# Spreading dt and du over the state rows: four DMAs of 32 channels over 128 partitions, or four DMAs of 128 channels over 32 partitions

## The reference

```python
def selective_scan(u, dt, Bm, Cm, A, Dp):
    def step(h, inp):
        u_t, dt_t, B_t, C_t = inp
        dA = jnp.exp(dt_t[..., None] * A)
        h = h * dA + (dt_t * u_t)[..., None] * B_t[:, None, :]
        y = jnp.einsum('bdn,bn->bd', h, C_t)
        return (h, y)
    ...
dt = jax.nn.softplus(x_dbl[..., :R] @ dt_w.T + dt_b)
Bm = x_dbl[..., R:R + N]
Cm = x_dbl[..., R + N:]
```

## Time and profile before

| what | us |
|---|---|
| median of 3 runs | 606.04 |
| profiled execution | 607.73 |
| its span | 605.9 |
| GpSimd busy | 517.9 (85%) |
| VectorE busy | 483.3 (80%) |
| TensorE busy | 480.8 (79%) |
| ScalarE busy | 357.5 (59%) |
| SP's DMA queue, share of 16 DMA engines | 47.6% |

### The profile page before, as it was taken

One profiled execution on the slowest core, in us unless ns is written; L12 is line 12 of the kernel. 1 busy time (PEld: TensorE's weight loads), 2 busy tenths in 40 slices (PEclk: granted clock), 3 DMA queues, 4 the chain that ended last, 5 costly groups with the idle time before them and its releaser, 6 DMA issues.

```text
span 605.9 us, 5758 instructions
## 1 busy us (share of the span) xinstructions
PE 480.8 (79%) x1679; PEld 177.7 (29%) x1679; DVE 483.3 (80%) x601; ACT 357.5 (59%) x634; POOL 517.9 (85%) x190
## 2 busy tenths in 40 slices
PE   2576858777788888869888888878887887888897
PEld 1232212232323232314232323232333223323243
DVE  2533069998989896999899889988998899799941
ACT  2454565758585856483857485848574764354533
POOL 5737159999999999999999999999999999989600
PEclk9997958899999897998998999999999998789999
DMA  6839458855555546564644864386429741900000
GB/s 66 33 32 183 84 133 199 192 148 123 152 121 147 130 141 138 144 140 143 138 110 116 190 159 108 98 189 178 109 78 187 195 114 45 207 3 10 9 1 17
DMA packets 51073, 71.32 MB, mean 118 GB/s; under 512 B 16434, under 2 KB 17378, under 8 KB 51042
## 3 DMA queue, kind: packets, MB, share of 16 engines
q1 hardware_dynamic: 48050, 69.63, 47.6%
q0 software_dynamic: 1024, 1.05, 4.5%
q10 hardware_dynamic: 1968, 0.29, 0.3%
HBM read 60.45 MB, written 10.49 MB: 117 GB/s over the span
## 4 chain that ended last, share of the span: by engine, by line
POOL 33%; issue 26%; PE 18%; DVE 15%; ACT 5%; DMA 2%; POOLq 0%; DVEq 0%; ACTq 0%
POOL st L464 16%; POOL st L455 12%; DVE st L1350 9%; DVE st L1337 3%; PE ps L580 2%; PE ps L640 2%; PE ps L646 2%; POOL l_ L441 2%; POOL dt L444 2%; DMA x<-in_L_tok_ple_table,idx 2%; PE ps L627 2%; PE ps L732 2%; PE ps L748 2%; POOL x L429 1%; PE ps L568 1%
## 5 line engine op out<-in xcount | busy, mean ns | idle before, releaser
L464 POOL TENSOR_TENSOR st<-st,repC 128x2048 f32<-128x2048 f32 x63 | 284.9, 4533 | 9.1 <-ACT carry L998 7.8
L1350 DVE TENSOR_TENSOR_SCAN st<-ps,carry,st 128x512 f32<-128x512 f32 x192 | 234.9, 1268 | 19.6 <-ACT carry L998 12.9
L992 ACT ACTIVATE ps<-dtS,negA 128x512 f32<-128x512 f32 x256 | 169.5, 681 | 51.8 <-DVE st L1350 50.4
L455 POOL TENSOR_TENSOR st<-duS,repB 128x2048 f32<-128x2048 f32 x31 | 140.5, 4531 | 0.5 <-PE ps L646 0.5
L640 PE MATMUL ps<-Bw,nought 128*128 128x512 f32 x194 | 103.6, 645 | 0.0
L646 PE MATMUL ps<-st,fold 128*32 128x512 f32 x504 | 69.5, 624 | 42.9 <-POOL st L464 42.7
L1350 DVE TENSOR_TENSOR_SCAN st<-ps,zero,st 128x512 f32<-128x512 f32 x64 | 78.1, 1267 | 3.8 <-POOL st L455 1.9
L1337 DVE TENSOR_TENSOR st<-duS,ps 128x2048 f32<-128x2048 f32 x33 | 75.0, 2271 | 6.3 <-PE ps L627 6.3
L580 PE MATMUL ps<-act,wT 128*128 128x512 f32 x128 | 62.4, 633 | 5.2 <-ACT act L943 5.2
L998 ACT ACTIVATE carry<-st 128x4 f32<-128x4 f32 x48 | 9.8, 204 | 77.7 <-DVE st L1350 77.5
L640 PEld LDWEIGHTS ps<-Bw,nought 128*128 128x128 f32 x194 | 35.6, 202 | 50.0 <-issue 49.9
(11 more groups left out here) (129 smaller groups left out, 590.4 us busy)
## 6 DMA issues: line engine op xcount, KB each, us to landing
dtS<-dt_dram SPq DMA_DIRECT2D x64, 256.0 KB, 6.9
duS<-du_dram SPq DMA_DIRECT2D x64, 256.0 KB, 4.6
repC<-bc_dram SPq DMA_DIRECT2D x64, 256.0 KB, 5.7
repB<-bc_dram SPq DMA_DIRECT2D x60, 128.0 KB, 2.9
dt_dram<-dt SPq DMA_DIRECT2D x16, 256.0 KB, 2.1
du_dram<-du SPq DMA_DIRECT2D x16, 256.0 KB, 2.0
bc_dram<-bc_sb SPq DMA_DIRECT2D x16, 64.0 KB, 5.5
out_h<-fin SPq DMA_DIRECT2D x8, 128.0 KB, 2.0
```

The costliest lines, as they stand in the source:

```text
L455: pool.tensor_tensor(st[:, r], duS[:, u % 2], row, ALU.mult).then_inc(sem("dbu_pool"), 1)
L464: pool.tensor_tensor(st[:, r], st[:, r], row, ALU.mult).then_inc(sem("hc_ready"), 1)
L992: sc.activation(decay_bank(u, r, q), dtS[:, u % 2, q], ACT.Exp, scale=negA[:, way(u), q, r:r + 1]).then_inc(sem("decay_ready"), 1)
L1350: dve.tensor_tensor_scan(st[:, r, q, order], decay_bank(u, r, q)[:, order], st[:, r, q, order], first, ALU.mult, ALU.add).then_inc(sem("sc ...
```

## The change

`load_dt` and `load_du` still issue four DMAs of 256 KB each for a unit. Before, the DMA for m writes all 128 channels (as 32 x 4 x 512) to the 32 partitions of that m. After, the DMA for q writes the 32 channels of that group to all 128 partitions, four copies of 32 rows; the source is a view of the DRAM rows with a leading dimension of 4 and step 0. The destination has 128 rows of 512 numbers. Waits, semaphores, buffers and the order of all instructions on all engines stay the same, and so do the bytes moved and the length of a contiguous piece (2 KB).

```diff
+            def four_times(of, u, q):
+
+                return of[u][32 * q:32 * q + 32].unsqueeze(0).broadcast_to([4, 32, T])
+
             def load_dt(u):
                 wait(sp, "decay_ready", NQ * NR * (u - 1))
                 sp.wait_ge(sem("dt_in_dram"), 16 * (u + 1))
-                for m in range(4):
-                    sp.dma_start(dtS[32 * m:32 * m + 32, u % 2], dt_dram[u].rearrange("(q d) t -> d q t", d=32)) \
-                      .then_inc(sem(f"dtS_in_{u % 2}"), 16)
+                for q in range(NQ):
+                    sp.dma_start(dtS[:, u % 2, q, :], four_times(dt_dram, u, q)).then_inc(sem(f"dtS_in_{u % 2}"), 16)
 
             def load_du(u):
                 ...
                 sp.wait_ge(sem("du_in_dram"), 16 * (u + 1))
-                for m in range(4):
-                    sp.dma_start(duS[32 * m:32 * m + 32, u % 2], du_dram[u].rearrange("(q d) t -> d q t", d=32)) \
-                      .then_inc(sem(f"duS_in_{u % 2}"), 16)
+                for q in range(NQ):
+                    sp.dma_start(duS[:, u % 2, q, :], four_times(du_dram, u, q)).then_inc(sem(f"duS_in_{u % 2}"), 16)
```

## The result

The changed kernel takes 697.72 us (median of 4 runs, 695.65 to 698.55), the kernel before on the same chip 606.21 us: 1.1506 times as long, 95% interval 1.148 to 1.1532. The profiled execution has a span of 696.1 us. The prediction was 761, range 648 to 915.

What follows compares the result with a forecast made beforehand. GpSimd bounds the kernel at 30.9 us a unit; on four engines SP's chain takes over. Unit 2's du loads at 128, 13 units of 41.5, 29.6 to dt's landing and 63.7 to the end give 761 us, range 648 to 915.

Steps and rivals of the forecast that it cites:

- GpSimd at 30.9 us a unit, 27 us of slack: Middle units: GpSimd's work sets 30.9 us a unit; readers of dtS and duS come some 27 us after the loads.
- The smaller side decides, four engines, the same four: New dt and du loads: source leads with 4, so each runs on the same 4 engines, 256 packets a unit; 84%.
- 31 missing small packets: SP's queue before: 5345 small packets against 336 x 16 = 5376, fitting three parameter DMAs with fewer than 16 rows.
- B: Rival on the new loads: all 16 engines are used and nothing changes, 606 us within 0.2%; chance 11%.
- C: Rival on the loads of units 0 and 1: all 16 engines and faster, at most 2 us gained, 604; chance 3%.
- D: Rival on the new loads: four engines, but not the same ones each time, 606 to 610 us; chance 2%.
- The chain of SP decides once it is over GpSimd's unit: SP's loads, bc store, repB and stores in sequence take 256p + 13.3 us a unit, over GpSimd's 30.9 even at 85 ns.
- The packet time: Time p of a 2 KB packet in the new loads: between 85 and 148 ns, 110 chosen.
- The remainder of the unit: SP's unit besides its 256 dt and du packets: repC, bc store, repB issue, stores, landings, gaps; 13.3 us including the start.
- The sum: Whole run: du loads of unit 2 at 128, 13 periods of 41.5, dt landing 29.6, end 63.7: span 760.8 us.
- The lower bound: The same sum with packets at 85 ns and units of 35.1 us: 665 us.
- The pairing of streams on ports: New loads' four write streams: in step they would pair on two ports at 148 ns, out of step run at 85.

Runs made afterwards that it cites:

- the series 2, 4, 8, 128: Changed kernel (source of dt and du loads leads with 4) with that dimension made 2, 8 or 128; ratios to the kernel before 1.671, 1.002, 0.9998.

## Why the prediction was right, and where its sizes were off

*GpSimd at 30.9 us a unit, 27 us of slack.* Right. With 16 engines and 128 rows the loads got faster and the time stayed.

*The smaller side decides, four engines, the same four.* Right, and now shown: 46514 packets, and the series 2, 4, 8, 128 gives 46258, 46514, 47026 and 48050. The forecast rested on 31 missing small packets in the trace of before. The Trainium skill ("DMA: Bandwidth & Descriptors", on why a DMA increments its semaphore by 16) takes the largest number up to 16 that divides the slowest dimensions of both sides. The trace agrees, on the destination side too, though all sizes tried are powers of two, for which that number and the smaller side are the same. Rivals B, C and D fall: D, since the share stays at four engines' through all eight loads, so that they don't run on different fours.

*The chain of SP decides once it is over GpSimd's unit.* Right: 158 us of waiting for the bc store, 39 for the du store, units of 36.8 us from unit 2 to 15, and no loss in the middle units where the chain is 30.1 us.

*The packet time: the step that was off.* I took 110 ns for all 256 packets. Measured is 84 ns alone, and 151 on the four engines in the stretch beside repC. The rows gave only the bounds, 85 and 148; 110 was a choice between them. The part from the issue of the du loads to the landing of dt is 373.1 - 346.22 = 26.9 us, where ScalarE's decay starts at once:

```profile
373.11 0.69 ACT L994 ACTIVATE ps<-dtS,negA 128x512 f32<-128x512 f32 x1 [5.62 <-DMA dtS<-dt_dram]
```

It is made of 2.3 for the start, 256 x 84 ns = 21.5, 0.5 for the landing (the prediction's estimate), and 2.6 left for the contention, where the count of packets above gave about 3.1. So the mean of the 256 packets is 94 ns, and not 110. I had 0.9 + 28.2 + 0.5 = 29.6: the start too short by 1.4, the packets too long by 4.1 with the contention counted. The remainder of the unit is 10.2 us; I had 13.3 less 1.4 = 11.9. So P, the length of a unit, was put at 41.5 and is 37.1 in this unit, 36.8 in the mean of 13.

*The sum.* Measured, from these rows (SP and ScalarE, answers the earlier trace rows):

```profile
125.70 2.50 SPq L360 DMA_DIRECT2D duS<-du_dram  x4
...
603.78 2.24 SPq L360 DMA_DIRECT2D duS<-du_dram  x4
```

```profile
631.57 0.69 ACT L994 ACTIVATE ps<-dtS,negA 128x512 f32<-128x512 f32 x1 [10.01 <-DMA dtS<-dt_dram]
```

125.7 (I had 128), 13 x 36.8 = 478.1 (539.5), 27.8 (29.6), end 696.1 - 631.57 = 64.5 (63.7): 696.1. Of the 65 us by which the predicted span was too long, 61 are the 13 units of 4.7 us. The lower bound, 665 at 85 ns, lacked the longer start and the contention: 1.4 + 2.6, less 1.7 for the remainder and 0.3 for the packets, is the 2.0 us between its unit of 35.1 and the 37.1 measured here.

*The pairing of streams on ports.* I had kept 148 ns open for four streams in step, by the Trainium skill ("SBUF — State Buffer", port swizzle). With nothing beside them, the four don't slow each other here: 84 ns, 98 GB/s together, the same 84 ns as with two engines. Either they run out of step or the pairing doesn't bite with four; no run tells which. That 16 engines on 32 partitions are slow is what the runs do show: 148 ns to 32 partitions, 90 ns to 128, both on 16 engines.

## What to carry to other kernels

Before a DMA's shape is changed, look at the leading dimension of both sides: with the sizes tried here, powers of two, the smaller one, up to 16, was the number of engines it ran on, and a copy made by a leading step of 0 counts as a dimension of its own, a small one. The count of small completion packets in a queue tells on how many engines its DMAs ran. A slow load with 27 us of slack still costs when it stands in one in-order queue ahead of small transfers that the issuer waits for; what counts is the length of that chain against the unit of the bounding engine, and while the chain is the shorter the loss is nearly nothing.

## What the runs showed of the hardware that I had not expected

- To 128 partitions a packet of 2 KB took 84 ns with two and with four engines at work and 90 ns with 16: 51, 98 and 369 GB/s.
- Loads to 32 partitions at a time on twelve engines slow the packets of the four others, which write to all 128: 151 ns a packet beside repC, about 160 beside dt and repC, 109 beside repC's loads to 128 partitions, 84 alone.
- The steady stream of a load on four engines began 2.3 us after the start of its issue, with eight packets alone at 1.3; on 16 engines the first packets came after 0.9 us and the full rate after 1.4. A store on four engines landed after 5.9 us, one on 16 after 2.0.
- SP's issue of a DMA grew to 2.4 us (9.54 for four) while its four engines had a backlog; before it was 0.43 in the middle of the kernel.
